# First stage of a graph network kernel: loads of 125 partitions cut into 112 and 13, another order of loads, first two matrices in pieces

## The reference

```python
q = (x @ Wq + bq).reshape(n, H, OUT_DIM)      # H = 4, OUT_DIM = 512
k = (x @ Wk + bk).reshape(n, H, OUT_DIM)
v = (x @ Wv + bv).reshape(n, H, OUT_DIM)
alpha = jnp.einsum('ehc,ehc->eh', q[dst], k[src]) / np.sqrt(OUT_DIM)
...
x_attn = agg + x @ Wskip + bskip
x_lin = x_attn @ Wlin + blin
```

## Time and profile before

| | |
|---|---|
| median of 3 runs | 2340.27 us (2334.76, 2340.27, 2343.05) |
| profiled execution | 2339.17 us, its span 2337.2 us |
| mean granted PE clock | 0.951 of full speed |
| PE busy | 2082.6 us, 89% of the span |
| DVE, ACT, POOL busy | 1334.8, 720.4, 378.0 us |
| block `prepare` | from 0 to about 236.5 us |

### The profile page before, as it was taken

One profiled execution on the slowest core, in us unless ns is written; L12 is line 12 of the kernel. 1 busy time (PEld: TensorE's weight loads), 2 busy tenths in 40 slices (PEclk: granted clock), 3 DMA queues, 4 the chain that ended last, 5 costly groups with the idle time before them and its releaser, 6 DMA issues. The chain is left out here.

```text
span 2337.2 us, 36737 instructions
## 1 busy us (share of the span) xinstructions
PE 2082.6 (89%) x13354; PEld 1817.8 (78%) x13355; DVE 1334.8 (57%) x3044; ACT 720.4 (31%) x1243; POOL 378.0 (16%) x317
## 2 busy tenths in 40 slices
PE   7876897899999999999998469999997999999576
PEld 5655665799989989998996349989886888888475
DVE  4544897344453444444433844566555888787667
ACT  3551101222222221222211022234234655565421
POOL 0000112000000000000000200111313544454443
PEclk9987998999999999999999789999997999999788
DMA  7651001213021211120001240021241021120542
GB/s 232 196 176 44 34 18 38 99 40 87 30 83 35 61 64 52 60 61 17 16 11 40 77 148 1 1 91 36 80 139 36 19 49 32 26 53 9 162 140 96
DMA packets 79015, 156.94 MB, mean 67 GB/s; under 512 B 7216, under 2 KB 22125, under 8 KB 77136
## 3 DMA queue, kind: packets, MB, share of 16 engines
q1 hardware_dynamic: 69340, 135.69, 19.3%
q0 software_dynamic: 4960, 11.49, 1.5%
q10 hardware_dynamic: 4616, 8.40, 1.0%
HBM read 104.19 MB, written 51.37 MB: 67 GB/s over the span
## 5 line engine op out<-in xcount | busy, mean ns | idle before, releaser
L130 PE MATMUL psum<-pt_hi,xn_hi 125*128 125x250 f32 x800 | 224.7, 281 | 1.6 <-DVE pt_lo L1065 1.6
L131 PE MATMUL psum<-pt_lo,xn_hi 125*128 125x250 f32 x800 | 223.7, 280 | 0.0
L132 PE MATMUL psum<-pt_hi,xn_lo 125*128 125x250 f32 x800 | 222.8, 279 | 0.0
L2146 POOL TENSOR_TENSOR mprob<-mprob,mrden 125x1250 f32<-125x1250 f32 x80 | 181.6, 2271 | 202.1 <-DVE mrden L2247 201.1
L130 PE MATMUL psum<-xt_hi,t_hi 128*125 128x512 f32 (+1 forms) x480 | 169.3, 353 | 2.8 <-DVE mx L1041 1.7
L131 PE MATMUL psum<-xt_lo,t_hi 128*125 128x512 f32 (+1 forms) x480 | 170.1, 354 | 0.0
L132 PE MATMUL psum<-xt_hi,t_lo 128*125 128x512 f32 (+1 forms) x480 | 169.8, 354 | 0.0
L967 ACT ACTIVATE prob<-prob,nb 125x1250 f32<-125x1250 f32 x40 | 53.6, 1341 | 346.6 <-DVE nb L1046 346.6
L1244 POOL TENSOR_TENSOR x_res<-x_res,beta 125x512 f32<-125x512 f32 x10 | 12.4, 1275 | 897.4 <-DMA x_res<-in_x 897.4
L2254 DVE TENSOR_REDUCE mmin<-psum 125x1 f32<-125x512 f32 (+1 forms) x240 | 127.2, 584 | 51.1 <-PE psum L2405 50.9
L2186 ACT ACTIVATE mprob<-psum,mbias 125x1250 f32<-125x1250 f32 x80 | 104.3, 1304 | 157.4 <-DVE mbias L2256 157.4
(11 more groups left out here) (497 smaller groups left out, 5802.1 us busy)
## 6 DMA issues: line engine op xcount, KB each, us to landing
slots_in<-slots_blank SPq DMA_DIRECT2D x12, 1282.5 KB, 10.6
cnt<-edge_counts SPq DMA_DIRECT2D x40, 305.2 KB
q_chunk<-q_store SPq DMA_DIRECT2D x40, 250.0 KB, 5.4
edge_attr<-in_attr SPq DMA_DIRECT2D x4, 1343.8 KB
slots_in<-slots_blank SPq DMA_DIRECT2D x3, 1539.0 KB, 18.4
moe_xg<-slots_in SPq DMA_DIRECT2D x17, 256.5 KB, 3.6
raw_WqT<-in_WqT SPq DMA_DIRECT2D x4, 1024.0 KB, 8.0
raw_WkT<-in_WkT SPq DMA_DIRECT2D x4, 1024.0 KB
```

The costliest lines, as they stand in the source:

```text
L130: nc.tensor.matmul(out, lh, rh, start=start, stop=False)
L131: nc.tensor.matmul(out, lh, rl, start=False, stop=False)
L132: return nc.tensor.matmul(out, ll, rh, start=False, stop=stop)
L2146: nc.gpsimd.tensor_tensor(prob[:, n % 4, :], prob[:, n % 4, :], rden[:, n % 4:n % 4 + 1].broadcast_to([P, N]), ALU.mult).then_inc(p_ready, 1)
```

## The change

Loads of x and of the edge attributes go through a new helper, `balanced`, that issues two transfers in place of one, for partitions 0 to 111 and 112 to 124; their semaphores are waited for at 32 in place of 16. Wq and Wk of head 0 come in four half loads (slices 0 and 1, slices 2 and 3), and ACT, DVE and PE treat these two matrices slice by slice for the first unit of the first product. Wv of head 0 is issued ahead of the biases and the edge rows. Attribute quarters 0 and 1 are issued at the end of head 0's loads, without a wait. The halves of x are issued ahead of the wait for the skip matrix of head 3, and not behind the load.

```diff
--- before.py
+++ after.py
@@ -241,6 +241,7 @@
     u_done, copied, added = sem("unit_done"), sem("unit_copied"), sem("unit_added")
     out_stored = [sem(f"product_stored{i}") for i in range(3)]
     lin_ready = sem("lin_ready")
+    first_in = [[sem(f"{names[i]}_first{half}") for half in range(2)] for i in (Q, K)]
     x_in, xs_ready = [sem("x_loaded0"), sem("x_loaded1")], sem("f0_xs")
     xt_done, xt_hi_done, xt_lo_done = sem("f0_xt"), sem("f0_xt_hi"), sem("f0_xt_lo")
     ln.turn += 1
@@ -274,7 +275,15 @@
         if i == LIN:
             eng.wait_ge(lin_in[h % 2], 16 * (h // 2) + 16)
         else:
-            eng.wait_ge(raw_in[i], 16 * h + 16)
+            eng.wait_ge(raw_in[i], 16 * h + (0 if i in (Q, K) else 16))
+
+    def split_count(i, h):
+        return h + KT if i in (Q, K) else h + 1
+
+    def balanced(sp, dst, src_, arrived):
+
+        for part in (slice(0, 112), slice(112, P)):
+            sp.dma_start(dst[part], src_[part]).then_inc(arrived, 16)
 
     def unit_of(h, kind, m):
 
@@ -291,41 +300,41 @@
                 sp.dma_start(raw_of(i, h)[:], block_of(i, h)).then_inc(arrived, 16)
 
             def attr_load(q):
-                sp.dma_start(ring[q % 2][:, 0:count[q], :], w["attr"][:, quarter[q], :]).then_inc(attr_in[q % 2], 16)
+                balanced(sp, ring[q % 2][:, 0:count[q], :], w["attr"][:, quarter[q], :], attr_in[q % 2])
 
             def x_half(s):
                 half = slice(0, NT // 2) if s == 0 else slice(NT // 2, NT)
-                sp.dma_start(x[:, half, :], tiles(w["x"])[:, half, :]).then_inc(x_in[s], 16)
-
-            matrix_in(Q, 0), matrix_in(K, 0)
+                balanced(sp, x[:, half, :], tiles(w["x"])[:, half, :], x_in[s])
+
+            for half in range(2):
+                cols = slice(2 * half, 2 * half + 2)
+                for i in (Q, K):
+                    sp.dma_start(raw[i][:, cols, :], block_of(i, 0)[:, cols, :]).then_inc(first_in[i][half], 16)
+            matrix_in(V, 0)
             for dst, name in ((g.bq[:], "bq"), (g.bk[:], "bk"), (bvs[:, 0, :], "bv"), (bvs[:, 1, :], "bskip")):
                 sp.dma_start(dst, w[name]).then_inc(cols_in, 16)
             sp.dma_start(dst_p[:], w["dst_groups"]).then_inc(s_load, 16)
             sp.dma_start(dst_i[:], w["dst_cols"]).then_inc(s_load, 16)
             sp.dma_start(src_i[:], w["src_cols"]).then_inc(s_load, 16)
-            matrix_in(V, 0), matrix_in(LIN, 0), matrix_in(SKIP, 0), matrix_in(LIN, 1)
+            matrix_in(LIN, 0), matrix_in(SKIP, 0), matrix_in(LIN, 1)
+            attr_load(0), attr_load(1)
             for h in range(1, HEADS):
                 sp.wait_ge(kq_rows, h)
                 matrix_in(Q, h), matrix_in(K, h)
-                if h == 1:
-                    attr_load(0)
                 sp.wait_ge(u_done, unit_of(h - 1, 2, 0))
                 matrix_in(V, h)
-                if h == 1:
-                    attr_load(1)
                 if h == 2:
                     for q in (2, 3):
                         sp.wait_ge(part_ready[q % 2], 3)
                         attr_load(q)
+                if h == HEADS - 1:
+                    for s in range(2):
+                        sp.wait_ge(part_ready[s], 6)
+                        x_half(s)
                 sp.wait_ge(u_done, unit_of(h, 0, 0))
                 matrix_in(SKIP, h)
                 if h + 1 < HEADS:
                     matrix_in(LIN, h + 1)
-                if h == HEADS - 1:
-                    sp.wait_ge(part_ready[0], 6)
-                    x_half(0)
-                    sp.wait_ge(part_ready[1], 6)
-                    x_half(1)
 
         @block.gpsimd
         def _(pool):
@@ -388,10 +397,14 @@
                 if n:
                     act.wait_ge(rest_ready[s], 2 * use + n)
                 else:
-                    act.wait_ge(attr_in[s], 16 * use + 16)
+                    act.wait_ge(attr_in[s], 32 * use + 32)
                 nc.scalar.activation(g.parts[:, quarter[q], n * EDGE_D:(n + 1) * EDGE_D], ring[s][:, 0:count[q], :], ACT.Copy).then_inc(part_ready[s], 1)
 
-            split_hi(Q, 0), split_hi(K, 0)
+            for k in range(KT):
+                for i in (Q, K):
+                    if k % 2 == 0:
+                        act.wait_ge(first_in[i][k // 2], 16)
+                    nc.scalar.activation(hi[i][:, k, :], raw[i][:, k, :], ACT.Copy).then_inc(hi_done[i], 1)
             bias_tops()
             split_hi(V, 0), split_hi(LIN, 0), split_hi(SKIP, 0)
             for m in range(KT):
@@ -446,7 +459,7 @@
             link = core.link.on(dve)
 
             def split_lo(i, h):
-                dve.wait_ge(hi_done[i], h + 1)
+                dve.wait_ge(hi_done[i], split_count(i, h))
                 nc.vector.tensor_tensor(lower(i, h)[:], raw_of(i, h)[:], f32(hi[i][:]), ALU.subtract).then_inc(lo_done[i], 1)
 
             def bias_rests():
@@ -473,7 +486,11 @@
                         last = nc.vector.tensor_tensor(g.gs_acc[:, m, :], g.gs_acc[:, m, :], unit_bank(m), ALU.add)
                     last.then_inc(added, 1)
 
-            split_lo(Q, 0), split_lo(K, 0)
+            for k in range(KT):
+                for i in (Q, K):
+                    dve.wait_ge(hi_done[i], k + 1)
+                    nc.vector.tensor_tensor(lo[i][:, k, :], raw[i][:, k, :], f32(hi[i][:, k, :]),
+                                            ALU.subtract).then_inc(lo_done[i], 1)
             bias_rests()
             dve.wait_ge(s_load, 48)
             dve.wait_ge(s_iota, 3)
@@ -518,7 +535,7 @@
                 split_lo(V, h + 1)
             split_lo(LIN, 3), split_lo(SKIP, 3)
             for s in range(2):
-                dve.wait_ge(x_in[s], 16)
+                dve.wait_ge(x_in[s], 32)
             normalise(nc, link, x, x, ln, ln.turn, xs_ready)
             for t in range(NT):
                 dve.wait_ge(xt_hi_done, t + 1)
@@ -554,12 +571,16 @@
                     pe.wait_ge(copied, 8 * h + (n - 4) % 12 + 1)
 
             def product(h, kind, i, j):
-                pe.wait_ge(lo_done[i], h + 1)
-                pe.wait_ge(lo_done[j], h + 1)
+                if h or kind:
+                    pe.wait_ge(lo_done[i], split_count(i, h))
+                    pe.wait_ge(lo_done[j], split_count(j, h))
                 left, right = (hi[i], lower(i, h)), (hi[j], lower(j, h))
                 for m in range(KT):
                     bank_free(unit_of(h, kind, m))
                     for k in range(KT):
+                        if h == kind == m == 0:
+                            pe.wait_ge(lo_done[i], k + 1)
+                            pe.wait_ge(lo_done[j], k + 1)
                         last = three_pass(nc, unit_bank(m), [a[:, k, m * 128:(m + 1) * 128] for a in left],
                                           [a[:, k, :] for a in right], k == 0, k == KT - 1)
                     last.then_inc(u_done, 1)
```

## The result

The changed kernel takes 2312.09 us (median of 4 runs, 2308.71 to 2314.93) against 2339.72 us before (4 runs, same chip): a ratio of 0.9887, interval 0.9872 to 0.9902. It is faster, by 27.6 us. The forecast was 2295 with a range of 2286 to 2307, so the direction was right and the time missed the range by 5 us. The profiled execution took 2314.93 us with a span of 2313.0 us.

What follows compares the result with a forecast made beforehand. PE, busy 89% of the span, was taken as the bound, so only its idle or slow places give time. 4.7 + 8.4 + 18.1 + 11.6 + 2.2 - 0.5 = 44.5 us off 2339.2 gave 2295, range 2286 to 2307.

Steps and rivals of the forecast that it cites:

- Part 1, the rate: Attribute and x loads as 112 and 13 partitions use 16 engines: an attribute load falls from 10.7 to 3.4 us.
- What the prediction quoted against two transfers over disjoint partitions: A skill page's rule on DMA loads: do not split one transfer over disjoint partitions, since both use the same engines and serialise.
- The cost: In head 0, attribute loads ahead of head 1's Q and K delay K, which has nearly no cover: 0.5 us charged.
- Heads 1 and 2: In the first block, both heads fall to 38.3 us each, as skip matrices land in time: 8.4 and 18.1 us gained.
- Part 2, x: At head 3, x issued before the skip matrix lands about 2 us into the head; PE's wait goes, 11.6 us gained.
- The 2.2 us between the first transposes: In head 3, ACT no longer has four product copies to make between the first two transpose pairs: 2.2 us gained.
- Part 3, the start: In head 0, PE starts at 9.0 and the second product at 27.3 instead of 32.0: 4.7 us gained.
- What PE gains here goes one for one into the span: The first block ends in a barrier for all engines, PE and DVE last, so PE's gain there shortens the span equally.
- B: Rival: head 1's Q and K come late, 5 to 10 us lost in head 0, time 2300 to 2305; chance 0.07.
- A: Rival: the split does not spread, parts run at 129 GB/s, only the order of loads acts; 2322 us; chance 0.07.
- C: Rival: gaps at the start hold PE at 1.2 GHz through head 0 into head 1; up to 2362 us; chance 0.03.
- D: Rival: no change, DVE or ACT sets an equally long new wait in each head; 2339 us; chance 0.03.

Runs made afterwards that it cites:

- b1: The changed kernel with edge attributes padded to 128 partitions and each quarter loaded by one transfer, x still in 112 and 13: 2300.26 us, ratio 0.9841 to before.
- a3: The changed kernel with the halves of x issued behind the skip matrix of head 3, as before: 2307.4 us, ratio 0.9866 to before.
- a2: The changed kernel with attribute quarters 0 and 1 issued in their old places: 2304.67 us, ratio 0.9851 to before.
- b4: The kernel before with only Q and K of head 0 in pieces and V ahead of the small loads: 2336.43 us, ratio 0.9998.
- c1: The kernel before with attributes on 128 partitions, x in 112 and 13 and the new order; Q and K whole, V in its old place: 2298.01 us, ratio 0.9833.
- d1: The kernel before with one probe group of four 128-partition loads ahead of its first loads, nothing else changed: 2349.96 us, one execution.
- d2: The kernel before with two probe groups of 128-partition loads ahead of its first loads, nothing else changed: 2372.37 us, one execution.
- a1: The changed kernel with each load of 125 partitions as one transfer again, new order kept: 2353.08 us, ratio 1.0058 to before.

## Why the prediction was wrong

**Part 1, the rate: this step failed.** It counted rows per engine ("8 in place of 25") and took the rate of 128 partitions for the rest: 3.4 us an attribute load. That all engines take part was right (share 0.99 with the split, 0.32 without), the rate was not: 235 GB/s, so 1343.8 KB take about 5.9 us. The named bounds, 129 and 391 GB/s, held the truth between them, but the sum took the upper end (3.4 us for a load is 405 GB/s). b1 shows that this is the step that failed: same order, attributes at full rate, block at 192.54 where the sum said 192.0, and 204.64 at the rate of 112 and 13. A half us is closer than the terms deserve, since b1's second product comes 0.9 us later than forecast and its head 0 is 0.6 shorter than charged.

What the prediction quoted against two transfers over disjoint partitions is not borne out here: one transfer of 125 moves 135 GB/s, 112 and 13 move 235, and the split alone gives 0.9845.

**The cost: mechanism right, size wrong.** The text saw that K has no cover in head 0 and charged 0.5 us; 7.9 are paid (5.3 in a3's profile of the same program: 56.28 - 27.13 - 23.85). K is split at 49.76, not 43, and ahead of it ACT waits 9.04 us for a store slot. The prediction had the stores only as 3 us on one engine that delay K, and not that the loads delay the stores. With the attributes later, a2, the time is 7.4 us shorter.

**Heads 1 and 2: right.** 8.4 and 18.1 us were forecast as a fall to 38.3 each. Measured: 38.30 and 38.40. It holds although the skip matrix of head 2 lands 12 us after its issue, not 6, and ACT waits 8.61 us: the cover is about that long. This slack is why the wrong rate did no harm inside these heads; ACT is late by it all the same, and x is issued late for head 3.

**Part 2, x: half right.** DVE's wait for x of 17.59 us is gone. But x went ahead of the skip matrix, and "SP reaches the skip matrix at T3 as before" overlooked that the DMA engines still carry x: ACT waits 9.36 us for it. DVE reaches x 19.7 us after T3 (155.81 - 136.10), not 10.8; PE idles 3.07. The premise that failed is the issue of x "some 5 us before T3": it came 1.7 before. In b1, with 6.4, head 3 takes what was forecast. The 2.2 us between the first transposes did not come: 164.80 to 169.59 is still 4.8, because ACT is so late that its four product copies stand ahead of the transposes' copies as before (163.00 to 166.75). In b1 3.2 us lie between them.

**Part 3, the start: right, and worth nothing in the time.** First matmul 8.76 (forecast 9.0), second product 27.62 (27.3). What it waited for last was not DVE's rest of Wlin, done at 26.90, but ACT's first product copy, done at 27.47 behind the split of the skip matrix; that the two lie 0.6 us apart is luck. b4 against before and c1 against b1 show no gain in the time, though their blocks end 7.8 and 4.1 us earlier: it is lost behind the block.

**"What PE gains here goes one for one into the span": not quite.** 31.9 us in the block gave 27.6 between the medians. d1 and d2 show that displacement alone changes the rest of the kernel by some us (2096.7 and 2104.1), with part of it in the return of the clock. That this accounts for the whole 4 us is argued, not shown.

**The rivals.** B named the mechanism, 5 to 10 us lost in head 0 (7.9 measured), at a chance of 0.07; its time of 2300 to 2305 lacks what head 3 and the stretch behind the block add. A's mechanism doesn't occur, but its time was checked by a1: 2353, not 2322. It left out that SP is blocked in issuing (9.17 and 11.82 us) and that ACT waits 22.39 us for the skip matrix in head 2. With unsplit loads the new order and the pieces together are a loss, a rival of the other sign that was not named. C's long slow stretch didn't occur: heads 1 and 2 run at 1.00, and so does head 0 of b1 from 28.20 on, with the same pieces; the 0.89 of after stands with its stalls. D didn't occur either.

## What to carry to other kernels

A DMA share near 1 is not full bandwidth: read the GB/s beside it, and when a load must be cut or padded, pad it to 128 partitions or measure the rate of the very rows that it writes (b1 against after: 12 us in the block). A load moved ahead of others is paid by all that stand behind it, stores of another queue too; look for their slack first, as heads 1 and 2 had it here and head 0 had not, and follow a late engine into the next head, since it also frees the places for the next loads. And weigh a start that comes earlier by the time of the whole kernel, not by its block: 7.8 us in b4's block were nothing at the end.

## What the hardware showed that was not expected

Sixty-four rows move at 407 GB/s on partitions 32 to 95 and at 202 to 212 on 0 to 63, 64 to 127 and 16 to 79, at a DMA share of about 1 each time. 120 rows (209 GB/s) are slower than 112 (276). A single issue on SP's queue can hold SP for 9 to 12 us when loads of 125 partitions are queued ahead of it (a1). A displacement of the same program by 15 us changes the stretch up to the output stage by 2 us, 1034.3 to 1036.2. And the same instructions of head 0 end 3 us apart from one execution to another (59.40 and 56.28).
